# Layer 2 of a two-layer kernel: the first expert's weights loaded in another order, router quarters added through transposes

## What is computed

```python
x = L0_attn_x                                  # (8, 256, 512): 2048 rows
xn = _layernorm(x, axis=-1)
s = _L0_attn_ref(xn, ...)                      # latent attention, 32 heads
g = _silu(_L0_ffn_ref(xn, ...))
x = x + s * g
xn = _layernorm(x, axis=-1)
s = _L1_attn_ref(xn)                           # attention across the batch
g = _silu(_L1_ffn_ref(xn, ...))                # experts
x = x + s * g

def _L1_attn_ref(x):                           # x: (8, 256, 512)
    q = jnp.transpose(x, (2, 0, 1))
    scores = jnp.einsum('lnc,lmc->lnm', q, q) / scale
    prob = jax.nn.softmax(scores, axis=-1)
    msg = jnp.einsum('lnm,lmc->lnc', prob, q)
    return x + jnp.transpose(msg, (1, 2, 0))

def _L1_ffn_ref(x, gate_w, w1, w2, w3):        # E = 8 experts, K = 2, F = 800
    logits = xt @ gate_w.T
    top_vals, top_idx = jax.lax.top_k(softmax(logits), K)
    top_vals = top_vals / jnp.sum(top_vals, axis=-1, keepdims=True)
    act = jax.nn.silu(xt @ w1.T) * (xt @ w3.T)     # each expert
    y = sum of w_full[t, e] * (act @ w2.T)
```

## Time and profile before

| | us |
|---|---|
| median of 3 runs | 1515.34 (1514.9 to 1516.48) |
| the profiled execution | 1513.35 |
| its span | 1511.4 |
| TensorE busy in the span | 1370.5 (91%) |
| VectorE, ScalarE, GpSimd busy | 701.2, 566.6, 614.9 |
| `across_batch`, from the profile's timeline | 772 to 887 |
| mean granted TensorE clock | 0.952 of full speed |

### The profile page before, as it was taken

The page is one execution under the profiler, slowest core; times in us unless marked ns, Lnnn a source line. Parts: engine busy times, 40 slices in busy tenths (PEclk is TensorE's granted clock), DMA queues, the critical chain, the costliest instruction groups (busy, mean ns, idle before and its releaser), DMA issues. The chain is left out here.

```text
span 1511.4 us, 25698 instructions
## 1 busy us (share of the span) xinstructions
PE 1370.5 (91%) x8190; PEld 1157.3 (77%) x8191; DVE 701.2 (46%) x1617; ACT 566.6 (37%) x1775; POOL 614.9 (41%) x516
## 2 busy tenths in 40 slices
PE   6989899999999999999867579999999999999940
PEld 6934487878778777878647479999999999999930
DVE  6452376666666666666546232222222222222236
ACT  3421365555555655556534222111112122122124
POOL 0010264544444445444425535071652617441135
PEclk9999999999999999999977689999999999999975
DMA  8025710000000000000013666173763728555247
GB/s 287 1 84 167 290 51 15 16 14 14 14 14 14 14 14 14 24 18 15 8 57 126 227 207 218 61 265 117 237 228 115 254 83 281 174 169 180 72 130 251
DMA packets 67069, 171.48 MB, mean 113 GB/s; under 512 B 6448, under 2 KB 15040, under 8 KB 66704
## 3 DMA queue, kind: packets, MB, share of 16 engines
q0 software_dynamic: 25776, 98.73, 19.6%
q1 hardware_dynamic: 35632, 61.95, 12.5%
q10 hardware_dynamic: 5616, 10.23, 1.9%
HBM read 125.26 MB, written 45.61 MB: 113 GB/s over the span
## 5 line engine op out<-in xcount | busy, mean ns | idle before, releaser
L1676 PE MATMUL bank<-expert_weights,rows_t 128*128 x1872 | 359.4, 347 | 2.0 <-DVE rows_t L1608 1.6
L1676 PEld LDWEIGHTS bank<-expert_weights,rows_t 128*128 128x128 f32 x1872 | 340.7, 189 | 6.0 <-issue 2.8
L953 ACT ACTIVATE room<-bank,room 128x256 f32<-128x256 f32 (+1 forms) x512 | 208.8, 415 | 114.6 <-DVE room L886 114.3
L981 POOL TENSOR_TENSOR room<-room 128x1024 f32<-128x1024 f32 (+1 forms) x128 | 187.9, 1468 | 121.3 <-DVE room L863 121.3
L735 PE MATMUL bank<-room 96*128 (+2 forms) x1024 | 232.5, 347 | 0.5 <-ACT room L953 0.4
L1620 DVE TENSOR_TENSOR x_keep<-x_keep,bank 128x400 f32<-128x400 f32 x78 | 44.5, 571 | 304.3 <-ACT x_keep L1563 303.0
L1088 POOL TENSOR_TENSOR expert_weights<-x_keep,expert_weights 128x1600 fp32r<-128x1600 f32 (+2 forms) x49 | 160.2, 3270 | 54.0 <-DMA expert_weights<-w 53.9
L735 PEld LDWEIGHTS bank<-room 96*128 96x128 f32 x1024 | 156.4, 192 | 28.5 <-issue 2.1
L988 POOL TENSOR_TENSOR room<-room 128x256 f32<-128x256 f32 x128 | 93.1, 728 | 186.8 <-DVE room L927 186.3
L1699 PE MATMUL bank<-expert_weights,act_t 128*128 x702 | 165.6, 389 | 1.0 <-ACT act_t L1568 1.0
L1699 PEld LDWEIGHTS bank<-expert_weights,act_t 128*128 128x128 f32 x702 | 131.5, 188 | 25.6 <-issue 1.3
(11 more groups left out here) (231 smaller groups left out, 1833.2 us busy)
## 6 DMA issues: line engine op xcount, KB each, us to landing
x_keep<-w POOLq DMA_DIRECT2D x28, 800.0 KB, 5.1
expert_weights<-w POOLq DMA_DIRECT2D x28, 800.0 KB, 6.7
x_keep<-w POOLq DMA_DIRECT2D x14, 768.0 KB, 5.7
expert_weights<-w POOLq DMA_DIRECT2D x14, 768.0 KB, 7.3
rows_by_expert<-room SPq DMA_DIRECT2D x1, 9984.0 KB, 28.6
x_keep<-rows_by_expert SPq DMA_DIRECT2D x39, 256.0 KB, 4.1
results_by_row<-x_keep ACTq DMA_DIRECT2D x39, 256.0 KB, 4.1
room<-wo SPq DMA_DIRECT2D x16, 512.0 KB, 5.9
```

Source lines behind the costliest of these rows:

```text
L953: last = sc.activation(Pr[:, m % 4, hh, 0:w], scores_bank(m)[:, w * hh:w * hh + w], ACT.Exp, bias=nb[:, par, hh:hh + 1], accum_out=sm[:, p ...
L981: g.tensor_tensor(pr, pr, rs[:, one[1] % 2].unsqueeze(2).broadcast_to([P, 4, w]), ALU.mult).then_inc(normed, 1)
L1676: last = mm(psum(2 * hf + w)[:, 0:HF], xgT[:, par, of_x, P * k:P * k + P], W[:, ds(off + (of_w * SLOT + (k * 2 + w) * FF + hf * HF), HF)], ...
```

## The change

`first_raw` has three buffers (chunk c in c % 3). SP loads chunks 0 to 2 at once and each later one when the low of the chunk three before it is made. The highs of chunks 0 to 2 are no longer made by ScalarE: GpSimd's queue issues three DMAs that convert on the way, straight into the weights' place (`high0_in`). GpSimd makes lows 0 to 3 ahead of its scatters, VectorE low 4 in round 1, and 5 and 6 stay in `experts`. ScalarE makes high 3 ahead of the router's exponential, 4 and 5 behind it and ahead of round 0, and 6 in round 1. `fold4` is gone: TensorE transposes `LT` tile by tile into four banks, and VectorE adds the quarters as it reads them; `turn_x(0)`, which writes one of these banks, waits for it (`p_ex`). VectorE's tables for the experts move into round 4 and count blocks with a chain of fused operations, not over a 39x7 product. Two semaphores of VectorE's rounds are replaced by its own chain semaphore.

```diff
-    ACT_HIGH, POOL_LOW, DVE_LOW = {0: 2, 1: 3, 3: 4, 4: 5, 6: 6}, (0, 1), {1: 2, 2: 3, 4: 4}
+    DMA_HIGH, POOL_LOW = range(3), range(4)
...
-    first_high, pool_low, dve_low, batched_p, batched_v = (sem(n) for n in (
-        "first_high", "pool_low", "dve_low", "batched_p", "batched_v"))
+    first_high, pool_low, batched_p, batched_v = (sem(n) for n in (
+        "first_high", "pool_low", "batched_p", "batched_v"))
+    high0_in = [sem(f"high0_in{c}") for c in DMA_HIGH]
...
     def raw_of(c):
         at, rows, n = CHUNKS[c]
-        return raw[0:rows, c % 2, 0:n]
+        return raw[0:rows, c % 3, 0:n]
...
             for c in range(NCH):
-                if c in (2, 3):
-                    sp.wait_ge(pool_low, c - 1)
-                if c >= 4:
-                    sp.wait_ge(dve_low, c - 3)
-                bring_chunk(sp, s, 0, c, raw[:, c % 2]).then_inc(s.raw0_in[c % 2], 16)
+                if c >= 3:
+                    sp.wait_ge(pool_low, c - 2)
+                bring_chunk(sp, s, 0, c, raw[:, c % 3]).then_inc(s.raw0_in[c % 3], 16)
...
+            for c in DMA_HIGH:
+                at, rows, n = CHUNKS[c]
+                bring_chunk(pool, s, 0, c, s.W[:, at:at + n]).then_inc(high0_in[c], 16)
...
             for c in POOL_LOW:
-                pool.wait_ge(first_high, c + 1)
+                if c in DMA_HIGH:
+                    pool.wait_ge(high0_in[c], 16)
+                else:
+                    pool.wait_ge(first_high, c - len(DMA_HIGH) + 1)
+                pool.wait_ge(s.raw0_in[c % 3], 16 * (c // 3 + 1))
                 low_of(s, c, raw_of(c), 0).then_inc(pool_low, 1)
...
             def high_of(c):
-                act.wait_ge(s.raw0_in[c % 2], 16 * (c // 2 + 1))
+                act.wait_ge(s.raw0_in[c % 3], 16 * (c // 3 + 1))
                 sc.activation(parts_of(s, c, 0)[HIGH], raw_of(c), ACT.Copy).then_inc(first_high, 1)
 
-            high_of(0)
+            high_of(3)
             act.wait_ge(p_ex, 1)
             sc.activation(p, p, ACT.Exp).then_inc(p_exd, 1)
-            high_of(1)
+            high_of(4)
+            high_of(5)
...
-                if r in ACT_HIGH:
-                    high_of(ACT_HIGH[r])
+                if r == 1:
+                    high_of(6)
...
+            for hf in range(2):
+                quarters = s.bank[2 + hf][:, :].rearrange("p (t k e) -> p t e k", t=NT // 2, k=4)[:, :, 0:E]
+                last = v.tensor_reduce(p[:, NT // 2 * hf:NT // 2 * hf + NT // 2], quarters, AX.X, ALU.add)
+                step(last)
+            step.wait()
             step.then(v.tensor_reduce(top, p, AX.X, ALU.max))
             v.tensor_tensor(p, p, top.unsqueeze(2).broadcast_to([P, NT, E]), ALU.subtract).then_inc(p_ex, 1)
             dve.wait_ge(p_exd, 1)
...
+            def block_tables():
+                ids = const("block_ids")
+                step(v.scalar_tensor_tensor(out=s.ends, in0=starts, scalar=1.0, in1=n_blocks, op0=ALU.add, op1=ALU.add))
+                step.then(v.tensor_scalar(of_block, ids, starts[:, 1:2], None, ALU.is_ge))
+                for e in range(2, E):
+                    step.then(v.scalar_tensor_tensor(out=of_block, in0=ids, scalar=starts[:, e:e + 1], in1=of_block,
+                                                     op0=ALU.is_ge, op1=ALU.add))
+                step(v.tensor_scalar(s.ready_at, of_block, float(len(CHUNKS)), 1.0, ALU.mult, ALU.add))
+
+                step.then(v.tensor_scalar(odd, of_block, 1.0, None, ALU.is_equal))
+                for k in (3.0, 5.0, 7.0):
+                    step.then(v.scalar_tensor_tensor(out=odd, in0=of_block, scalar=k, in1=odd, op0=ALU.is_equal,
+                                                     op1=ALU.add))
+                step(v.tensor_scalar(s.slot_at, odd, 2.0 * SLOT, None, ALU.mult))
...
                     dve.wait_ge(a_scored, r + 1)
-                    v.tensor_reduce(mx[:, r % 2], psum(2 + r % 2).rearrange("p (g k) -> p g k", g=4), AX.X,
-                                    ALU.max).then_inc(a_maxed, 1)
-                    dve.wait_ge(a_maxed, r + 1)
+                    step.then(v.tensor_reduce(mx[:, r % 2], psum(2 + r % 2).rearrange("p (g k) -> p g k", g=4), AX.X,
+                                              ALU.max))
                     v.tensor_scalar(nb[:, r % 2], mx[:, r % 2], -INV, None, ALU.mult).then_inc(a_bias, 1)
                     dve.wait_ge(a_xt, 2 * r + 2)
                     if r >= 3:
                         dve.wait_ge(a_msg, 2 * (r - 2))
                     v.tensor_copy(xg[:, r % 3, 1], psum(5).rearrange("p (g c) -> p g c", g=4)).then_inc(a_xt_v, 1)
                     dve.wait_ge(a_exp, r + 1)
-                    v.reciprocal(rc[:, r % 2], sm[:, r % 2]).then_inc(a_recip, 1)
-                    dve.wait_ge(a_recip, r + 1)
+                    step.then(v.reciprocal(rc[:, r % 2], sm[:, r % 2]))
                     v.tensor_tensor(pr[:, r % 3], pr[:, r % 3], rc[:, r % 2].unsqueeze(2).broadcast_to([P, 4, P]),
                                     ALU.mult).then_inc(a_norm, 1)
-                if r in DVE_LOW:
-                    c = DVE_LOW[r]
-                    high, low = parts_of(s, c, 0)
-                    dve.wait_ge(first_high, c + 1)
-                    v.tensor_tensor(low, raw_of(c), high, ALU.subtract).then_inc(dve_low, 1)
-
-
-            step(v.scalar_tensor_tensor(out=s.ends, in0=starts, scalar=1.0, in1=n_blocks, op0=ALU.add, op1=ALU.add))
-            step.then(v.tensor_tensor(which, const("block_ids").unsqueeze(2).broadcast_to([P, NBLK, E - 1]),
-                                      starts[:, 1:E].unsqueeze(1).broadcast_to([P, NBLK, E - 1]), ALU.is_ge))
-            step.then(v.tensor_reduce(of_block, which, AX.X, ALU.add))
-            step(v.tensor_scalar(s.ready_at, of_block, float(len(CHUNKS)), 1.0, ALU.mult, ALU.add))
-
-            step.then(v.tensor_scalar(odd, of_block, 1.0, None, ALU.is_equal))
-            for k in (3.0, 5.0, 7.0):
-                step.then(v.scalar_tensor_tensor(out=odd, in0=of_block, scalar=k, in1=odd, op0=ALU.is_equal,
-                                                 op1=ALU.add))
-            step(v.tensor_scalar(s.slot_at, odd, 2.0 * SLOT, None, ALU.mult))
+                if r == 1:
+                    high, low = parts_of(s, 4, 0)
+                    dve.wait_ge(first_high, 2)
+                    v.tensor_tensor(low, raw_of(4), high, ALU.subtract)
+                if r == 4:
+                    block_tables()
...
-            pe.wait_ge(consts2_in, 16)
             for t in range(NT):
                 pe.wait_ge(logit_out, t // 4 + 1)
-                last = mm(psum(7)[:, E * t:E * t + E], LT[:, P * t:P * t + P], const("fold4"), start=True, stop=True)
+                last = tr(psum(4 + t // 4)[:, P * (t % 4):P * (t % 4) + P], LT[:, P * t:P * t + P], ident)
             last.then_inc(lt, 1)
 
...
             score(0)
+            pe.wait_ge(p_ex, 1)
             turn_x(0)
```

17 lines of the change are left out of this document (7 added, 10 removed).

## The result

The changed kernel takes 1521.05 us (median; 1516.89 to 1522.73), the kernel before, run beside it, 1515.38 (1512.72 to 1522.06). The ratio is 1.003, 95% interval 1.0022 to 1.0039: slower by 3.3 to 5.9 us, where 1508.5 was forecast, and outside the range. The profiled execution of the changed kernel has a span of 1516.2 us.

A forecast was written before the change was run, and what follows sets the result against it. Two chains were taken to bound layer 2's attention stage: router, slots, scatters, and a VectorE tail. Terms -3.0 (a to c), -1.8 (d), -1.8 (f) gave -6.6 us, 1508.5 against a median of 1515.34; range 1488 to 1514.

The forecast's parts named there:

- (a): Router fold on TensorE, ahead of the slots: 16 transposes replace 16 calls, 5.98 to 3.3 us, -2.6 us.
- (b): VectorE's reading of the logits: two reductions in place of a copy, +0.6 us (0.3 to 0.9).
- (c): VectorE's router chain: GpSimd's low of chunk 1 leaves, chunk 3's comes, -1.4 us; with (a), (b) -3.0 for slots_ready.
- Rival C: Ahead of the rounds, GpSimd's lows shut out VectorE's eight copies and eat the gain: 1512.7 to 1515.7 us; chance 0.11.
- (d): Length of the 32 scatters: one VectorE low of three left beside them, -1.8 us, if the scatters still bound.
- (e): Weight loads no longer beside the scatters: added transfers and highs cost nothing, effect on the stall likeliest zero.
- case A: The forecast: the stall in the rounds is the scatters' own and ends with them, 4.8 us earlier; chance 0.43.
- Rival B: Without loads beside the scatters the stall in the rounds shrinks or goes: 1488 us, half of it 1498; chance 0.33.
- Rival D: Store of messages goes at 829, stall sets in a round or two sooner: 1519.5, up to 1526 us; chance 0.13.
- (f): Tail of the stage: block tables no longer behind the last message, so the barrier opens sooner, -1.8 us.
- A stall of 24.6 us: Layer 2's attention rounds: scores of rounds 5 and 6 start late against the 5.4 us pace, the stage's largest single loss.

The follow-up runs named there:

- fold alone: The kernel before with only the new router fold (transposes, quarters added on read): 1491.95 us, ratio 0.9992.
- Late lows: The changed kernel, GpSimd's lows waiting for VectorE's eight copies of rows: 1490.43 us, ratio 0.9985 to the kernel before; on another chip 1517.01, 1.0008.
- tables alone: The kernel before with only block_tables moved to round 4: 1492.31 us, ratio 0.9996; on another chip 1518.22, 1.0023.
- loads alone: The changed kernel with the old fold and the tables at the end: 1496.36 us, ratio 1.002 to the kernel before; on another chip 1524.32, 1.0065.

## Why the prediction was wrong, point by point

- **(a), (b)** held in size. The fold fell from 5.98 to 3.15 us (forecast 3.3), and the two reductions took 0.76. That a shorter fold brings the slots forward by its length did not hold by itself: in fold alone 4.0 us of it gave 0.4.
- **(c)**, and with it the -3.0 of (a) to (c), is the first step that failed: slots_ready came 0.9 us later. The lock in the router chain, which (c) prices, did shrink, by 2.0 us where it says 1.4. What failed is what the sum put at nothing: the three lows beside the normalising, which set the start of the fold back by 5.2 us. Rival C had the mechanism, GpSimd's lows against VectorE, and sized it at 1512.7 to 1515.7, but looked for it at the eight copies alone. The copies begin at 786.30 and the lows were expected from 784, so the last normalising operations could have been seen to overlap them. The lock sat there, and cost 10.4 us where the forecast counted some 9 of idle time. Late lows show it: 10.3 us, and slots 3.0 us sooner than with the lock, 1.8 sooner than before, inside the term's own bounds (1 to 4.5). The Trainium skill, "SBUF — State Buffer", section "Who interferes with whom", counts tensor_scalar as well as copy among the operations that can take the shared port. By that rule the row of normalising should have been priced. The trace agrees that such an operation can be locked, with 3.85 us for one tile; that it ran in the two-port mode which the section asks for fits an unlocked tile's 0.53 us, between a copy (0.42) and a tensor_tensor (0.69) of the same shape, but isn't shown.
- **(d)** held in size: from the first scatter to the last 42.06 us before, 40.30 after, -1.8. It was worth nothing, because the rounds, not the scatters, ended the stage.
- **(e)** "in the likeliest case zero" is the step that cost the sign. That the scatters by themselves hold up TensorE's signals, case A, was right on the chips that have the hole. The conclusion that the hole would then only move with them was not: with the loads gone from beside the scatters it opened 5 to 6 us sooner against the first scatter. One round fewer was done ahead of the hole and was done behind it, 5.9 us. Rival B, that without loads the hole may go, had the sign of the loads' effect wrong; that they held it off by interrupting the scatters is the likely reason, not a shown one.
- **Rival D** came out in its time (1519.5 to 1526) and its size (a round or more moved behind the stall), with another cause: no store of messages ran before 862 us. Its condition, round 3's scores not yet out, was set too strictly; they were out at 828.3, and their signal was seen at 837.5.
- **(f)** was worth nothing (6.26 and 6.44 us from the last sum to the experts). It looked at the barrier alone. The next transfer stands on SP's queue behind the last store of messages, which still left with the last sum. In round 4 the tables cost 3.6 us where that round was the one held up (tables alone), 0.5 in the changed kernel.
- A stall of 24.6 us that no instruction explains was taken as given, the same on every chip. It is not.
- Two slips in the sum change nothing: 1515.34 - 6.6 is 1508.7, not 1508.5, and 5.98 - 3.3 is 2.7, not 2.6.

## What to carry to other kernels

Ask of every operation that is moved beside GpSimd's work what VectorE does in all that time, not only at the place where the last trace showed a lock, and ask of a removed transfer whom it had held up: that may have been a service. Where a long row of indirect DMAs delays an engine's signals, tie their issue to that engine: two lines on top of late lows gave 19 us against the kernel before on a chip that needed it, and the tie cost 1 to 4 us on one that didn't. Compare kernels on one chip only: here the chips differ by 22 us and the change by 6. A barrier that opens sooner is worth nothing while the next stage's load waits in a queue behind an old store.

## What the runs showed of the hardware

- GpSimd's 32 indirect scatters (50% of the DMA engines) delay TensorE's signals by up to 30.7 us (loads alone) in three comparisons; plain stores of the same bytes, at 94% and issued in 17 us, don't, and on three other chips the scatters don't either (the kernel before takes 1492 to 1493 there, not 1514 to 1516). In the hole TensorE also gets its own instructions slowly: between single matmuls of 0.27 to 0.37 us it stands idle for 1.0 to 2.5 us. ScalarE's signal to TensorE came at once in the same hole (copy done at 843.02, matmul at 843.08). What is shared there, and what differs between the chips, stays open.
- Six pauses of 0.9 to 2.9 us, four scatters apart, keep the delay of every signal whose record is there at 2.0 us or less.
- A normalising operation, 0.53 to 0.54 us when alone, that runs while GpSimd subtracts takes as long as that subtraction, 3.78 to 3.89 us; 16 of them took 20.1 to 20.2 us in every trace of a kernel with the early lows but two, of 16.9 us.
- `across_batch` starts at 770.3 to 776.3 us in the traces, though the code ahead of it is the same, so a single trace can't tell 2 us by its end; counted from the stage's start it can.
